# A decoder layer on one core: expert weights split by GpSimd during the self attention, and position scores stored by sequence, then head

## The reference

```python
x = _layernorm(x + attn(x))          # 16 heads of 8, learned relative positions, softmax
x = _layernorm(x + xattn(x, ctx))    # 16 heads of 8, causal, keys and values from ctx
x = _layernorm(x + ffn(x))           # experts: 64 of them, 8 chosen per token, and a shared one

# in attn: logits = q k^T * scale + pos[b, h], pos from q and rel_emb by relative distance
# in ffn:
tidx, tw = _route(x, router_w, correction_bias)
combine = zeros((T, E)).at[arange(T)[:, None], tidx].add(tw)
for e in range(64):
    routed += combine[:, e, None] * (relu2(x @ up_w[e]) @ down_w[e])
shared = relu2(x @ shared_up_w) @ shared_down_w
```

## Time and profile before

| | |
|---|---|
| time, median of 3 runs | 279.58 us (279.5 to 280.51) |
| time of the profiled execution | 279.9 us |
| its span | 278.1 us |
| PE busy, 1912 matmuls | 254.1 us |
| DVE busy | 202.9 us |
| ACT busy | 215.5 us |
| POOL busy | 142.0 us |
| chain that ended last | PE 58%, DVE 13%, POOL 9%, SPq 5%, DMA 4%, ACT 3% |

### The profile page before, as it was taken

How to read it: one execution, slowest core, us unless ns; L and a number is a source line. 1 busy time by engine, 2 the same in 40 slices (tenths; PEclk the granted TensorE clock), 3 DMA queues, 4 the chain that set the end, 5 groups by cost and what they waited for, 6 DMA issues and landing times.

```text
span 278.1 us, 5979 instructions
## 1 busy us (share of the span) xinstructions
PE 254.1 (91%) x1912; PEld 202.5 (73%) x1912; DVE 202.9 (73%) x563; ACT 215.5 (77%) x572; POOL 142.0 (51%) x137
## 2 busy tenths in 40 slices
PE   4989999999999999998896769999998999999991
PEld 3679998788888877776664445668886888788860
DVE  2698736778888889997999973588995457844424
ACT  8572661889999989999998776688897887698861
POOL 5018002400111159654654004488998998699982
PEclk9999999999999999999999988999999999999997
DMA  6719320597623316756660002976581698497201
GB/s 129 179 41 409 102 60 2 142 248 250 176 81 87 97 49 133 181 164 181 171 182 1 1 2 61 244 187 171 179 223 37 166 241 199 142 231 195 78 0 38
DMA packets 52259, 37.94 MB, mean 136 GB/s; under 512 B 15810, under 2 KB 43140, under 8 KB 52228
## 3 DMA queue, kind: packets, MB, share of 16 engines
q1 hardware_dynamic: 52228, 37.57, 50.8%
HBM read 30.48 MB, written 7.08 MB: 135 GB/s over the span
## 4 chain that ended last, share of the span: by engine, by line
PE 58%; DVE 13%; POOL 9%; issue 7%; SPq 5%; DMA 4%; ACT 3%; DVEq 0%; POOLq 0%; ACTq 0%
PE bank L741 20%; PE bank L723 10%; POOL unit_lo L644 6%; PE bank L758 5%; PE bank L776 5%; PE bank L786 4%; PE bank L764 3%; SPq L461 3%; DVE neg_max L1245 3%; PE bank L672 2%; DMA qc_dram<-q_lo 2%; SPq L457 2%; PE bank L679 1%; PE bank L803 1%; DVE scaled L1376 1%
## 5 line engine op out<-in xcount | busy, mean ns | idle before, releaser
L644 POOL TENSOR_TENSOR unit_lo<-unit,unit_hi 128x512 fp32r<-128x512 f32 x68 | 86.5, 1298 | 32.9 <-ACT unit_hi L1093 31.9
L1001 ACT ACTIVATE probs<-bank,neg_max 128x128 f32<-128x128 f32 x224 | 63.9, 395 | 4.5 <-DVE neg_max L1245 4.3
L1376 DVE SCALAR_TENSOR_TENSOR scaled<-bank,roots 128x512 f32<-128x512 f32 x64 | 43.8, 686 | 27.6 <-PE bank L741 22.8
L1092 ACT ACTIVATE unit<-scaled 128x512 f32<-128x512 f32 x68 | 42.9, 630 | 17.2 <-DVE scaled L1376 15.5
L1245 DVE TENSOR_REDUCE neg_max<-bank 128x4 f32<-128x512 f32 x56 | 38.3, 685 | 10.9 <-PE bank L764 10.3
L1093 ACT ACTIVATE unit_hi<-scaled 128x512 fp32r<-128x512 f32 x68 | 42.0, 617 | 0.0
L776 PE MATMUL bank<-ident,probs 128*128 128x128 f32 x256 | 39.0, 275 | 3.1 <-ACT probs L1001 3.1
L776 PEld LDWEIGHTS bank<-ident,probs 128*128 128x128 f32 x256 | 30.1, 140 | 8.5 <-ACT probs L1001 5.4
L764 PE MATMUL bank<-k_bd,q_stk 128*128 128x512 f32 x64 | 34.0, 532 | 0.0
L723 PE MATMUL bank<-spread,rel_t 128*128 128x128 f32 x256 | 28.9, 275 | 0.0
L723 PEld LDWEIGHTS bank<-spread,rel_t 128*128 128x128 f32 x256 | 28.7, 192 | 0.1
(11 more groups left out here) (212 smaller groups left out, 479.4 us busy)
## 6 DMA issues: line engine op xcount, KB each, us to landing
roots<-root_dram SPq DMA_DIRECT2D x60, 256.0 KB, 4.7
q_stk<-q_dram SPq DMA_DIRECT2D x16, 128.0 KB, 3.0
k_bd<-k_dram SPq DMA_DIRECT2D x32, 64.0 KB, 2.3
incoming<-in_L_ffn_up_w SPq DMA_DIRECT2D x4, 512.0 KB, 4.6
q_stk<-qc_dram SPq DMA_DIRECT2D x16, 128.0 KB, 3.1
k_bd<-kc_dram SPq DMA_DIRECT2D x32, 64.0 KB, 2.5
incoming<-in_L_ffn_down_w SPq DMA_DIRECT2D x4, 512.0 KB, 4.5
k_dram<-k_hi SPq DMA_DIRECT2D x2, 512.0 KB, 3.4
```

Of the source, the lines that this page charges most:

```text
L644: nc.gpsimd.tensor_tensor(unit_lo[:, k % R], unit[:, k % 3], unit_hi[:, k % R], ALU.subtract).then_inc(lo_ready, 1)
L1001: last = nc.scalar.activation(probs[:, U % 3, h4 * L:(h4 + 1) * L], ps[BS[U % 3]][:, h4 * L:(h4 + 1) * L], ACT.Exp, bias=neg_max[:, U % 4, ...
L1092: nc.scalar.activation(unit[:, k % 3], scaled[:, k % 3], ACT.Square)
L1376: ins = nc.vector.scalar_tensor_tensor(scaled[:, k % 3], h, 0.0, roots[:, n % ROOT_RING, c % ROOTS], ALU.max, ALU.mult)
```

## The change

Rows of `pos` are stored as `b * H + h` instead of `h * NB + b`: the rows of sequence b are now 16 neighbours, 8 KB, done with once block b has its scores. `w_hi` and `w_lo` become one tensor `w_parts`, in which piece n has its two parts side by side, 8 KB, over exactly the rows of sequence n. So GpSimd's split of piece B waits for the scores of block B (`scores_ready` NG * (B + 1)) and goes into iteration B instead of B + 8. SyncE loads piece n in iteration B = n + 2 instead of n + 7. The split of the shared weights moves to GpSimd's iteration 0. The products read their weights through `expert_weights`.

```diff
--- before.py
+++ after.py
@@ -116,6 +116,13 @@
     return n // (NB // 2), slice(n % (NB // 2) * size, (n % (NB // 2) + 1) * size)
 
 
+def expert_weights(w_parts, way, c):
+
+    per_piece = 2 * NPAIR // NB
+    cols = slice(c % per_piece * 128, (c % per_piece + 1) * 128)
+    return [w_parts[:, way * NB // 2 + c // per_piece, part, cols] for part in range(2)]
+
+
 def h_bank(k):
 
     return (0, 1)[k % 2] if k < NSH + EARLY else BH[k % len(BH)]
@@ -184,8 +191,7 @@
 
         q_spread = spread[:, :].rearrange("p (r i n) -> p r i n", r=2, i=32)
 
-        w_hi = sb("w_hi", [128, 2, E * IM], F32R)
-        w_lo = sb("w_lo", [128, 2, E * IM], F32R)
+        w_parts = sb("w_parts", [128, NB, 2, 2 * E * IM // NB], F32R)
         x2_hi = sb("x2_hi", [128, NB * L], F32R)
         x2_lo = sb("x2_lo", [128, NB * L], F32R)
         sh_hi = sb("sh_hi", [128, 2, NSH * 128], F32R)
@@ -389,6 +395,10 @@
         stored = sem("stored")
 
         block = ctx.enter_context(nc.Block())
+
+        def pos_rows(n):
+
+            return pos[:, :, 4 * n:4 * n + 4].rearrange("p (b h) i -> p h b i", h=H)
 
         def bank_of(task):
             return ps[PREP_BANKS[TASKS.index(task) % len(PREP_BANKS)]]
@@ -510,8 +520,8 @@
                     sp.wait_ge(qc_split, 2 * (b + 1))
                     keep(qc_dram, (0,), q_hi, cols, qc_kept[b % 2])
                     keep(qc_dram, (1,), q_lo, cols, qc_kept[b % 2])
-                if 2 <= B - 7 < NB:
-                    load_piece(B - 7)
+                if 2 <= B - 2 < NB:
+                    load_piece(B - 2)
             for f in range(2):
 
                 cols = slice(f * HT, (f + 1) * HT)
@@ -611,21 +621,19 @@
                     pool.wait_ge(qc_split, 2 * b + 1)
                     nc.gpsimd.tensor_tensor(q_lo[:, cols].bitcast(F32R), q_t[:, cols], q_hi[:, cols], ALU.subtract)\
                         .then_inc(qc_split, 1)
-                if B >= NB:
-                    b = B - NB
-                    if b == 0:
-                        pool.wait_ge(ld["sup"], 16)
-                        pool.wait_ge(ld["sdn"], 16)
-                        pool.wait_ge(scores_ready, NU)
-                        pool.wait_ge(kc_kept, 16 * REPS)
-                        nc.gpsimd.tensor_copy(sh_hi[:, :, :], shared[:, :, :]).then_inc(shared_high, 1)
-                        pool.wait_ge(shared_high, 1)
-                        nc.gpsimd.tensor_tensor(sh_lo[:, :, :], shared[:, :, :], sh_hi[:, :, :], ALU.subtract)
-                    way, cols = piece(b)
-                    pool.wait_ge(ld[f"piece{b % 2}"], 16 * (b // 2 + 1))
-                    nc.gpsimd.tensor_copy(w_hi[:, way, cols], incoming[:, b % 2]).then_inc(w_high, 1)
-                    pool.wait_ge(w_high, b + 1)
-                    nc.gpsimd.tensor_tensor(w_lo[:, way, cols], incoming[:, b % 2], w_hi[:, way, cols],
+                if B == 0:
+                    pool.wait_ge(ld["sup"], 16)
+                    pool.wait_ge(ld["sdn"], 16)
+                    nc.gpsimd.tensor_copy(sh_hi[:, :, :], shared[:, :, :]).then_inc(shared_high, 1)
+                    pool.wait_ge(shared_high, 1)
+                    nc.gpsimd.tensor_tensor(sh_lo[:, :, :], shared[:, :, :], sh_hi[:, :, :], ALU.subtract)
+                if B < NB:
+
+                    pool.wait_ge(ld[f"piece{B % 2}"], 16 * (B // 2 + 1))
+                    pool.wait_ge(scores_ready, NG * (B + 1))
+                    nc.gpsimd.tensor_copy(w_parts[:, B, 0], incoming[:, B % 2]).then_inc(w_high, 1)
+                    pool.wait_ge(w_high, B + 1)
+                    nc.gpsimd.tensor_tensor(w_parts[:, B, 1], incoming[:, B % 2], w_parts[:, B, 0],
                                             ALU.subtract).then_inc(w_split, 1)
 
             for k in range(-1, 2 * CH):
@@ -754,7 +762,7 @@
                 if U < NU:
 
                     for h4 in range(GH):
-                        row = head_of(g, h4) * NB + b
+                        row = b * H + head_of(g, h4)
                         nc.tensor.matmul(bank[:, h4 * L:(h4 + 1) * L], pos[:, row, :], ident[:, :],
                                          start=(h4 == 0), stop=False, is_transpose=True, skip_group_check=True)
                 else:
@@ -858,7 +866,7 @@
                 if k == NSH:
                     pe.wait_ge(w_split, NB)
                 if c >= 0:
-                    w = [t[:, 0, c * 128:(c + 1) * 128] for t in (w_hi, w_lo)]
+                    w = expert_weights(w_parts, 0, c)
                 else:
                     w = [t[:, 0, (c + NSH) * 128:(c + NSH + 1) * 128] for t in (sh_hi, sh_lo)]
                 product(ps[h_bank(k)][:, :], w, [t[:, f * HT:(f + 1) * HT] for t in (x2_hi, x2_lo)],
@@ -883,7 +891,7 @@
                 if k == CH:
                     pe.wait_ge(ct_out, 2)
                 if c >= 0:
-                    w = [t[:, 1, c * 128:(c + 1) * 128] for t in (w_hi, w_lo)]
+                    w = expert_weights(w_parts, 1, c)
                 else:
                     w = [t[:, 1, (c + NSH) * 128:(c + NSH + 1) * 128] for t in (sh_hi, sh_lo)]
                 product(ps[(BO, BN)[f]][:, :], w, (unit_hi[:, k % R], unit_lo[:, k % R]), c == -NSH,
@@ -983,8 +991,8 @@
             nc.scalar.copy(k_hi[:, :].bitcast(F32R), k_t[:, :]).then_inc(k_high, 1)
             for n in range(L // 4):
                 if not by_vector(f"bias{n}"):
-                    nc.scalar.copy(pos[:, :, 4 * n:4 * n + 4],
-                                   done(f"bias{n}").rearrange("p (i r) -> p r i", i=4)).then_inc(out_a, 1)
+                    nc.scalar.copy(pos_rows(n), done(f"bias{n}").rearrange("p (i h b) -> p h b i", i=4, h=H))\
+                        .then_inc(out_a, 1)
             act.wait_ge(k_kept, 16 * REPS)
             nc.scalar.mul(kc_t[:, 0:HT], done("kc0"), SCALE).then_inc(out_a, 1)
             nc.scalar.mul(kc_t[:, HT:], done("kc1"), SCALE).then_inc(out_a, 1)
@@ -1208,9 +1216,9 @@
                                         .broadcast_to([128, HB, H, HD]), ALU.add).then_inc(out_v, 1)
 
             def bias_out(n):
-                nc.vector.tensor_tensor(pos[:, :, 4 * n:4 * n + 4], done(f"bias{n}").rearrange("p (i r) -> p r i", i=4),
-                                        rel_mask[:, 4 * n:4 * n + 4].unsqueeze(1).broadcast_to([128, H * NB, 4]),
-                                        ALU.add).then_inc(out_v, 1)
+                nc.vector.tensor_tensor(pos_rows(n), done(f"bias{n}").rearrange("p (i h b) -> p h b i", i=4, h=H),
+                                        rel_mask[:, 4 * n:4 * n + 4].unsqueeze(1).unsqueeze(1)
+                                        .broadcast_to([128, H, NB, 4]), ALU.add).then_inc(out_v, 1)
 
             dve.wait_ge(out_a, out_count("q0", False))
             spread_queries(0)
```

## The result

The changed kernel takes 288.24 us (median of 4, 287.21 to 289.81) against 280.04 us for the kernel before, measured beside it: ratio 1.0281, 95% interval 1.0241 to 1.032. That is 2.8% slower, +8.2 us where I forecast +3.6 and a range up to 287.0. The sign and the loop were forecast right, the size was not.

What follows compares the result with a forecast made beforehand. SyncE's in-order queue, 6.2 us a block, was barely below the engines' pace; a new 10.0 us loop would bind. Block 12's 4.2 late + 0.6 slow issues - 1.2 r_one = +3.6: 283.2 us, range 279.9 to 287.0.

Steps and rivals of the forecast that it cites:

- The loop and its turn: SyncE and GpSimd, keeps 0 to 3: piece transfer 4.6, split 3.5, queries 0.8, keep 1.1; 10.0 us a block.
- The loop's start: SyncE's queue after the kc keeps: two gathers of 4.7 to 4.8 us, piece 4 at 78.2, keep 0 at 87.1.
- Gather 11: Cross attention: block 11 begins 5.63 us after its gather starts, at 125.1; slower k_bd issues add 0.3 us a gather.
- Block 12 from the queue alone: After keep 3 only SyncE's queue counts: gather 12 at 125.65, block 12 at 131.3, 4.2 us late.
- clock rival: TensorE idles some 3.5 us before block 11, its clock falls, about 1.5 us more: 284.7 us; chance 10%.
- main case: The loop delays blocks 10 to 12 of the cross attention: +3.6 us, own range 281.5 to 285; chance 56%.
- Later blocks keep this distance: Blocks after 12 keep the delay, with the queue at 6.2 us a block and the engines at 6.6 to 7.2.
- r_one, -1.2 us: First routing operation on VectorE, 1.45 us at 133.35, becomes short once GpSimd's splits are gone: -1.2 us.
- The lock on the way in: Self attention: layer norms may wait for GpSimd's splits, nothing to 0.9 us a hit, perhaps two of five; taken as nothing.
- a self attention longer than 53 us: Sign that the forecast is wrong: the VectorE and GpSimd port lock would cost what was put at nothing.
- The storage order: Copies and adds into pos on ScalarE and VectorE: same elements and runs, so no change in time.
- The wait that goes: SyncE no longer waits 6.5 us for the first split; alone this also removes the 1.03 us idle at block 12.

Runs made afterwards that it cites:

- first two experiments: Changed kernel with GpSimd splitting queries B-3, not B-5, before piece B: 280.33 us, 0.9983; changed kernel with SyncE loading the piece before the keep: 281.84 us, 1.0042.
- small pieces: Changed kernel with pieces 2 and 3 loaded for only an eighth of their columns: 285.03 us, ratio 1.0162.
- quartered run: Changed kernel with each GpSimd weight split cut into quarters of 256 columns, order untouched: 290.19 us, ratio 1.031.
- quarters with the queries first: Changed kernel with GpSimd splitting queries B-3, not B-5, before piece B, and each weight split cut into quarters: 279.32 us, ratio 0.9948.

## Why the prediction was wrong, point by point

The reference points are the profiled executions, and block 12; from there to block 15 the distance is constant.

- **The loop and its turn: right.** 10.0 us forecast, 29.5 for three turns measured. The first two experiments show it is the cause.
- **The loop's start: the step that failed, and the largest miss, 3.5 us.** "two gathers follow, each 4.7 to 4.8 us" took the durations of a queue without pieces in it. With 512 KB ahead, gather 5 took 7.0 (gather 6 kept to 4.7), piece 2 landed after 6.8 us, and keep 0 came at 90.6 for 87.1. Half a microsecond of it is that the last write of keys ended at 68.15 for 67.66. The small pieces show it: 3.2 us of the time.
- **Gather 11: +1.2 us.** "its block 5.63 us after that" was 6.8 here (122.10 to 128.92), its four k_bd issues 3.73 us for 2.56. I had +0.3 a gather on the mean; it fell on the one gather where nothing hid it.
- **Block 12 from the queue alone: +1.3 us.** "From there the queue alone counts" gave block 12 at 5.63 us after gather 12, from its measured start at 129.47 that is 135.1. It began at 136.38, because block 11 took 7.5 us to go through after the gap, TensorE working all of it at a granted clock of 0.79. That was the clock rival, at its place and with about its price of 1.5; I had held it to be an alternative to the main case, and it came on top.
- **Against that, 0.8 us too much:** three turns half a microsecond shorter, the keep's landing 2.09 for 2.35. Sum: 4.2 + 3.5 + 1.2 + 1.3 - 0.8 = 9.4, measured 9.3 (136.38 less 127.05).
- **From 9.3 at block 12 to 7.3 at the end of the span: not in the forecast.** "Later blocks keep this distance" held to block 15. Then 1.8 us came back, 1.2 of them where the granted clock was 0.64 before and 1.00 after. The miss in the time is smaller for it, by luck.
- **r_one, -1.2 us: mis-sized.** It became 0.22 us. From block 12 to block 15 it was 20.5 us against 20.75. Forecast "on VectorE, which has no gap from there", but after the change ScalarE had none either: in the profile's stretch 140 to 150 it works all 10.00 us, VectorE 9.19. I read it so that the gain of one engine stopped at the other; no run tests it.
- **The lock on the way in, taken as nothing: right at the end, wrong in the stage.** It cost the self attention 3 us. The bounds, "to 0.9 us a hit, perhaps two hits of five", were too low: three hits, of 0.5, 1.2 and 1.4. The rows of the quartered run show that the loop hid it. The forecast's sign for this, a self attention longer than 53 us, came true (48.73 to 103.84 is 55.1), without its meaning for the end.
- **A reading that changed nothing:** "the keeps lay far ahead of their use" does not hold for keep 3 before, at 111.46 with its gather at 113.81. The queries came early, but the keeps stood right ahead of their gathers, as the 2.35 us of the sum has it.
- **The storage order, nothing: right,** shown alone.
- **The wait that goes:** I gave it 1.03 us. Alone in the kernel before it brought nothing (1.0, 0.9969 to 1.0032); together with the early splits, 0.5% by the ratio of the quarters with the queries first.

The range failed because it took the rivals as exclusive: crowding, the long gather and the lower clock behind the gap came together. The changed kernel with the queries' splits in order of time and in quarters takes 0.5% less than the kernel before (0.9929 to 0.9967); with whole splits one of two runs shows a gain (0.9957, 0.9925 to 0.9988), the other none (0.9983, 0.9949 to 1.0018).

## What to carry to other kernels

When work is moved forward on one in-order queue, look at what now stands behind it: here it was 0.8 us of queries behind a piece that another queue loads only after the queries of the sequence before, and the two queues then went round a loop of 10 us where 6.2 were wanted. Write such a loop down hop by hop, and take each hop's length from a stretch as crowded as the new one will be. The stall of 4.1 us on TensorE had an aftermath of 1.3 us at a lower clock; such a cost is added to the stall and not kept as an alternative to it.

## What the runs showed of the hardware

- A gather could start 1.7 us after the issue of the 64 KB write to DRAM that it waited for, with nothing large directly ahead of that write, and 4.4 us after it with a 512 KB load directly ahead in the same queue.
- Issuing took longer behind a large load: two q_stk issues took 1.2 us in a quiet stretch, and at gather 5 3.74 behind a piece, 1.91 behind an eighth of one, 2.15 with none (the kernel before, at 67.70). At gather 6 a piece ahead made 2.12.
- A layer norm of 0.34 us took up to 2.42 when a GpSimd TENSOR_TENSOR began 10 ns ahead of it; an input stride of two elements changed neither the 0.34 nor the waiting. The 11 executions of one kernel spread from 278.6 to 286.0 us, and the longest, the one profiled, had three such meetings.
- Behind a gap of 4.09 us TensorE's granted clock was 0.50 over 131 to 133 us, the lower of its two levels (1.2 and 2.4 GHz), and 1.00 again over 137 to 139; the block behind the gap took 7.5 us for 6.2.
